# Routing in the attention loop: one TensorE product turns a row block back and gives its router logits, and VectorE adds the bias

## The reference

```
h = _layernorm(x) * (1 + cb) + sb
scores = softmax(h @ Wr + br)
_, top_idx = top_k(scores, 2)
weights = softmax(where(chosen, scores, -inf))
out = sum over the two experts of weights * (gelu(h @ W1 + b1) @ W2 + b2)
```

## Time and profile before

| | |
|---|---|
| median of three runs | 1105.14 us |
| span of the profiled execution | 1104.4 us |
| PE busy | 1019.0 us, 92% |
| DVE busy | 923.8 us, 84% |
| ACT busy | 969.8 us, 88% |
| POOL busy | 825.8 us, 75% |
| attention phase | about 30 to 815 us |
| granted PE clock from 60 to 800 us | 1.00 of full speed, 2.4 GHz |

### The profile page before, as it was taken

How to read it: one execution, slowest core, us unless ns; L and a number is a source line. 1 busy time by engine, 2 the same in 40 slices (tenths; PEclk the granted TensorE clock), 3 DMA queues, 4 the chain that set the end, 5 groups by cost and what they waited for, 6 DMA issues and landing times. The chain is left out here.

```text
span 1104.4 us, 27346 instructions
## 1 busy us (share of the span) xinstructions
PE 1019.0 (92%) x7434; PEld 791.3 (72%) x7434; DVE 923.8 (84%) x2706; ACT 969.8 (88%) x3517; POOL 825.8 (75%) x1197
## 2 busy tenths in 40 slices
PE   5899999999999999999999999999989999999800
PEld 3478888888888888888888888888865455579600
DVE  4888999989999999888888888888766997778837
ACT  6899999999999999999999999999769999999534
POOL 6665578888888888888878788888745687777744
PEclk9999999999999999999999999999999999999955
DMA  5320000001000000000000000000034233321158
GB/s 150 104 71 14 13 18 23 23 26 34 27 23 26 26 23 14 16 16 16 14 15 16 14 14 16 16 16 16 16 111 129 84 118 104 96 85 40 46 207 261
DMA packets 53704, 57.90 MB, mean 52 GB/s; under 512 B 7964, under 2 KB 42639, under 8 KB 53556
## 3 DMA queue, kind: packets, MB, share of 16 engines
q1 hardware_dynamic: 36468, 35.10, 10.9%
q0 software_dynamic: 8640, 16.87, 4.4%
q10 hardware_dynamic: 8448, 4.20, 1.3%
HBM read 33.08 MB, written 23.97 MB: 52 GB/s over the span
## 5 line engine op out<-in xcount | busy, mean ns | idle before, releaser
L751 ACT ACTIVATE squares<-unit 128x128 f32<-128x128 f32 x1024 | 273.0, 302 | 3.6 <-PE unit L1211 3.4
L563 POOL TENSOR_TENSOR roped<-roped,rope_b 128x512 f32<-128x512 f32 x132 | 174.9, 1326 | 93.8 <-DVE rope_b L1099 91.4
L751 ACT ACTIVATION_READ_ACCUMULATOR squares<-unit 128x1 f32 x1024 | 234.1, 235 | 0.0
L1080 DVE TENSOR_TENSOR roped<-unit,cos_sb 128x512 f32<-128x512 f32 x256 | 174.4, 681 | 31.7 <-ACT squares L751 30.9
L1563 POOL DMA_INDIRECT y_rows<-y_out,place_y x142 | 155.3, 1093 | 54.3 <-issue 40.5
L1099 DVE TENSOR_TENSOR rope_b<-unit,sin_sb 128x512 f32<-128x512 f32 x256 | 174.3, 681 | 0.0
L729 ACT ACTIVATE probs<-scores,rr 128x256 f32<-128x256 f32 x256 | 123.7, 483 | 51.6 <-issue 25.5
L1291 PEld LDWEIGHTS unit<-ident,roped 128*128 128x128 f32 x1024 | 117.9, 142 | 31.9 <-ACT k_t L768 13.1
L1049 DVE SCALAR_TENSOR_TENSOR acc<-pv,den,acc 128x128 f32<-128x128 f32 x448 | 139.0, 341 | 0.3
L1291 PE MATMUL unit<-ident,roped 128*128 128x128 f32 x1024 | 135.2, 275 | 1.7 <-POOL roped L563 1.6
L572 POOL TENSOR_TENSOR roped<-roped,rr 128x1024 f32<-128x1024 f32 x64 | 121.6, 1900 | 9.6 <-DVE roped L1108 8.8
(11 more groups left out here) (310 smaller groups left out, 2972.3 us busy)
## 6 DMA issues: line engine op xcount, KB each, us to landing
shared<-y_rows SPq DMA_DIRECT2D x16, 512.0 KB, 5.6
x_all<-in_L_attn_x SPq DMA_DIRECT2D x32, 128.0 KB, 2.1
h_late<-in_L_ffn_W SPq DMA_DIRECT2D x16, 256.0 KB, 3.5
out_x<-hidden ACTq DMA_DIRECT2D x16, 256.0 KB, 4.4
rope_b<-x_rows SPq DMA_DIRECT2D x13, 258.0 KB, 2.9
tile_x<-x_rows SPq DMA_DIRECT2D x12, 258.0 KB, 3.0
y_rows<-y_out,place_y POOLq DMA_INDIRECT x142, 2.3
ga_b<-mod_dram SPq DMA_DIRECT2D x32, 64.0 KB, 2.9
```

Source lines behind the costliest of these rows:

```text
L563: pool.tensor_tensor(out=roped[parity][:, u, heads], in0=roped[parity][:, u, heads], in1=rope_b[:, u % 2, heads], op=ALU.add)\
L751: nc.scalar.activation(squares[:, c * D:(c + 1) * D], UN[0][:, c * D:(c + 1) * D], ACT.Square, accum_out=ssq[parity][:, u * H + c:u * H + ...
L1080: nc.vector.tensor_tensor(out=roped[parity][:, u, heads].rearrange("p (g c) -> p g c", c=D // 2), in0=UN[0][:, heads].rearrange("p (g c) - ...
```

## The change

One product per 128-token block replaces three kinds of PE work. Its moving operand is a 128 x 136 tile, `ident_wr`, the identity with Wr beside it, so its output holds the turned block in columns 0 to 127 and the logits without bias in columns 128 to 135. Both products are issued right ahead of the values of heads 0 and 1, in slots 1 and 2, into columns 376 to 511 of banks pv0 and pv1. They stay there until `copy_rows` reads them, which remains in slots 4 and 5. DVE adds the bias with a new tile `br_all` (br on all partitions, one more DMA at the start) and writes the logits to a new SBUF tile `lg`; the steps behind read `lg`. In the code before they read PSUM. `ROUTE` moves several steps, ACT's exponential moves from slot 2 to slot 3, and POOL computes `h_lo` before `score`. Five small DVE instructions that split br at the start go.

```diff
+        lg = sb("lg", [P, TT, E])
...
-        BESIDE, TURN_AT = 2 * P + 8, 3 * P
+        BESIDE, TURN_AT = 2 * P + 8, 3 * P - E
...
+        ROUTED = {1: 0, 2: 1}
...
             ROUTE = {
-                (1, 0): (TOP_L0, TOP_L1), (1, 1): (LESS_TOP,), (3, 3): (E_SUM,), (3, 4): (E_REC,),
-                (5, 0): (TOP_S0, TOP_S1), (5, 1): (TOP_I0,), (5, 2): (TOP_I1,),
+                (1, 1): (BIASED0,), (2, 0): (BIASED1,), (2, 1): (TOP_L0, TOP_L1), (2, 3): (LESS_TOP,),
+                (4, 0): (E_SUM,), (4, 1): (E_REC,), (5, 1): (TOP_S0, TOP_S1), (5, 2): (TOP_I0,), (5, 3): (TOP_I1,),
                 (6, 1): (ONE_HOT,)}
...
-                    lg = OP[0][:, BESIDE:BESIDE + TT * E].rearrange("p (t e) -> p t e", t=TT)
...
+                    if step in (BIASED0, BIASED1):
+                        t = step - BIASED0
+                        wait(dve, "rt_done", TT * b + t + 1)
+                        ins = nc.vector.tensor_tensor(out=lg[:, t, :], in0=OP[t][:, TURN_AT + P:TURN_AT + P + E],
+                                                      in1=br_all[:, :], op=ALU.add)
...
                     elif step == LESS_TOP:
...
-                        ins = nc.vector.tensor_tensor(out=lg_m[:, :, :], in0=lg,
+                        ins = nc.vector.tensor_tensor(out=lg_m[:, :, :], in0=lg[:, :, :],
                                                       in1=top_l[:, :, 0:1].to_broadcast([P, TT, E]), op=ALU.subtract)
...
-                    if RT and h + 1 in BACK_AT:
-                        t = BACK_AT[h + 1]
+                    if RT and h + 1 in ROUTED:
+                        t = ROUTED[h + 1]
                         wait(pe, "h2t_copied", n - 4)
-                        nc.tensor.transpose(o[:, TURN_AT:TURN_AT + P], h2_t[:, t * P:(t + 1) * P], ident[:, :])\
-                            .then_inc(S["h2_back"], 1)
+                        wait(pe, "rows_copied", TT * (n - 5))
+                        wait(pe, "route_step", STEPS * (n - 6) + BIASED1)
+                        nc.tensor.matmul(o[:, TURN_AT:TURN_AT + P + E], h2_t[:, t * P:(t + 1) * P], ident_wr[:, :],
+                                         start=True, stop=True).then_inc(S["rt_done"], 1)
...
-                        for k in range(3):
-                            nc.tensor.matmul(dst, ones_bf[0:1, :], br_part[k][:, :], start=(k == 0), stop=False)
-                        for t in range(TT):
-                            ins = nc.tensor.matmul(dst[:, t * E:(t + 1) * E], h2_t[:, t * P:(t + 1) * P], wr_sb[:, :],
-                                                   start=False, stop=(t == TT - 1))
...
-                    if C and RT and h == 3:
-                        wait(pe, "route_step", STEPS * (n - 5) + LESS_TOP)
+                    if C and RT and h in (3, 4):
+                        wait(pe, "route_step", STEPS * (n - 5) + (BIASED0, BIASED1)[h - 3])
```

More of the change, by code:

```diff
@@ L98, in adaln_block @@
         mod_t = sb("mod_t", [P, 4, NB])
-        wr_sb = sb("wr_sb", [P, E])
         br_sb = sb("br_sb", [1, TT * E])
-        br_rest = [sb(f"br_rest{k}", [1, TT * E]) for k in range(2)]
-        br_part = [sb(f"br_part{k}", [1, TT * E], BF16) for k in range(3)]
+        br_all = sb("br_all", [P, E])
         ones_row = sb("ones_row", [1, P])
@@ L293, in iterations @@
                 body(n // 2, n % 2, live(n))
-        (TOP_L0, TOP_L1, LESS_TOP, E_SUM, E_REC, TOP_S0, TOP_S1, TOP_I0, TOP_I1, ONE_HOT) = range(1, 11)
+        (BIASED0, BIASED1, TOP_L0, TOP_L1, LESS_TOP, E_SUM, E_REC, TOP_S0, TOP_S1, TOP_I0, TOP_I1, ONE_HOT) = range(1, 13)
         STEPS = ONE_HOT
@@ L628, in body @@
                     scatter(n - 6, parity, 0, 0)
+                if X:
+                    b = n + 1
+                    wait(pool, "hhi_done", b + 1)
+                    wait(pool, "vw_done", TT * (b - 1))
+                    pool.tensor_tensor(out=h_lo[other][:, :], in0=h_t[:, :], in1=h_hi[other][:, :], op=ALU.subtract)\
+                        .then_inc(S["h_ready"], 1)
                 if RT:
@@ L634, in body @@
                                        op=ALU.mult).then_inc(S["scored"], 1)
[L635 to L640, removed]
                 if A:
@@ L777, in body @@
                             .then_inc(S["guess_done"], 1)
-                    if RT and h == 2:
+                    if RT and h == 3:
                         b = n - 5
@@ L819, in body @@
                         if not late:
-                            wait(act, "rt_done", b)
-                            wait(act, "h2_back", TT * b)
+                            wait(act, "rt_done", TT * b)
                         nc.scalar.activation(h2_late[:, b - LAST, :] if late else h2_t[:, :], UN[1][:, 0:T],
@@ L880, in biases @@
             def biases():
[L882 to L890, removed]
+                dve.wait_ge(S["router_in"], 16 * (TT + 2))
                 dve.wait_ge(S["b_turned"], 1)
@@ L956, in after @@
                         own(dve, "route_step", at + k)
-                    lg = OP[0][:, BESIDE:BESIDE + TT * E].rearrange("p (t e) -> p t e", t=TT)
-                    if step in (TOP_L0, TOP_L1):
+                    if step in (BIASED0, BIASED1):
[3 more added lines that the diff above has]
+                                                      in1=br_all[:, :], op=ALU.add)
+                    elif step in (TOP_L0, TOP_L1):
                         t = step - TOP_L0
-                        if t == 0:
-                            alone(dve, "rt_done", b + 1)
+                        after(BIASED0 + t)
                         ins = nc.vector.max(top_l[:, t, :], lg[:, t, :])
@@ L1022, in copy_rows @@
                     b, t = n - 5, BACK_AT[h]
-                    wait(dve, "h2_back", TT * b + h - H_AT + 1)
+                    wait(dve, "rt_done", TT * b + t + 1)
                     if (not isinstance(b, int) or b >= 2) and h == H_AT:
```

22 lines of the change are left out of this document (8 added, 14 removed).

## The result

The changed kernel is slower: 1118.09 us as the median of four runs (1117.49 to 1120.25), against 1105.7 us for the kernel before in the same comparison (1104.69 to 1106.32). The ratio is 1.0116, with an interval from 1.0104 to 1.0129. The forecast was 1099.6 us, faster, with a range of 1090 to 1117. The profiled span is 1116.5 us, 12.1 more than before.

A forecast was written before the change was run, and what follows sets the result against it. PE was taken to set the 24.56 us round, with a DVE and POOL ring equally long; -0.15 us in 25 rounds (-3.8) and -0.55 in three (-1.7) gave -5.5: 1098.9 in the profiled span, 1099.6 against the median, range 1090 to 1117.

The forecast's parts named there:

- PE's saving: PE, each routing round: -0.80 for small products, -0.22 for turns, +0.47 for new products; net -0.55 us (-0.58 to -0.42).
- rival (d): PE: small passes were nearly free, so the change saves no PE time; 1105 us, chance 0.04.
- The ring: DVE and POOL wait on each other in 24.56 us; PE's lead of 0.15 shrinks that to about 24.41.
- the slack of the earlier trace: Rounds from 19 on: DVE waits for ACT ahead of L1080 in slot 4, 0.36 us in round 25.
- The timing of the subtraction: DVE, slot 2: subtraction at 423.47, POOL's scaling L572 at 423.57 in round 17; late rounds counted on POOL being as late.
- DVE is first by 0.1 us, and the subtraction passes: Slot 2: the subtraction, with both inputs in SBUF, starts before POOL's L572 and is not held by the shared port.
- Rival (b): Slot 2: L572 holds the subtraction in all rounds from 7 on; +10 us, 1115, chance 0.22.
- the rounds that gain 0.55: Rounds 5, 6 and 32, without the scatter, gain PE's full 0.55 us each: -1.7 us in all.
- (a): PE stays the bound because the DVE and POOL waits fall elsewhere; 28 x -0.55 = -15.4 us, 1089, chance 0.15.
- (c): Slot 2: L572 holds the subtraction in the late rounds alone; +1 us, 1106, chance 0.17.
- Two other terms: Moved routing steps neither lengthen nor shorten DVE's dense stretch; PE's new waits name work DVE has already finished.

The follow-up runs named there:

- last experiment: Changed kernel with logits in PSUM, fourth scatter behind the first scaling and L620, first layer-norm statistics in slot 3 instead of 4: 1124.71 us, ratio 0.9878.
- first experiment: Changed kernel with the biased logits in spare columns of PSUM bank pv0 instead of the SBUF tile: 1130.65 us, ratio 0.993 against the kernel before.
- two more edits: On the changed kernel with logits in PSUM: fourth scatter moved behind the first scaling (ratio 0.9928), then also first statistics in slot 3 (0.9878).

## Why the prediction was wrong

- **PE's saving was right.** A pass of 136 columns takes 0.12 us (two passes, 0.24 from 422.45 to 422.69) against 0.117 forecast. Rounds 5 and 6, where nothing is held, are 0.40 us shorter in the changed kernel, not the 0.55 that I gave them, for some of PE's wait at heads 6 and 7 is there too; with the chain around it loosened the round is 0.52 to 0.56 us shorter (last experiment) against 0.55. That small float32 passes are not nearly free, the bet against rival (d), held.
- **The ring was right in kind.** I said that DVE and POOL would set the round and PE would wait for `acc` ahead of head 7. With the hold taken out (first experiment), the early round is 24.40 against 24.41 forecast, PE waits for `acc` ahead of head 7 (433.57), and POOL's L515 (L517 there) takes 0.55 us instead of 0.67. The late rounds were mis-sized: 24.19 instead of 24.41, so there the slack of the earlier trace rows let through 0.37 and not 0.15. With the hold in, PE waits first for L1096, in slots 4 and 5, a link that I hadn't named.
- **The timing of the subtraction was right in the early rounds.** I forecast a lead of 0.10 us over the scaling; it was 0.14 (428.82 against 428.96), and 0.13 in the first experiment, whose round has the forecast length. In rounds 19 to 30 the scaling came first, by 0.07 us. The forecast rested there on POOL being as late as in round 17, without a row for it.
- **The step that failed is "DVE is first by 0.1 us, and the subtraction passes".** I took the listed start of L572 as the moment at which it takes the lock. The instruction ahead of it is a scatter; with the scaling ready behind that, VectorE was refused 0.14 to 0.61 us before the scaling's listed start, the scatter then being 0.4 to 0.9 us under way. Two runs with 0.4 and 0.5 us of lead were held for the whole scaling; the run whose scaling was not yet free was not. No row of before showed this, since in none had a VectorE instruction with two SBUF inputs fallen into that gap. The nearest one misleads: the L1108 at 417.17 began 0.91 us into a scatter and 0.12 us ahead of the small L515, and passed in 0.69 us. I had not asked what POOL's instruction ahead of L572 was, and gave the forecast 0.42 on a margin of 0.1 us.
- **Rival (b) is what happened**, by its mechanism, with a chance of 0.22. It put the early round at 25.2, measured 25.13, and the late ones 0.25 to 0.4 over today, measured 0.35. Its sum of +10 came out as +12.1 in the span. The early rounds cost 6.8 us for 7.8, rounds 5 and 6 gave 0.8 for 1.1, and round 32, which I had put among the rounds that gain 0.55, lost 2.1: the subtraction stays held through both scalings there, 4.60 us. That this is the cause has no experiment of its own; where round 32 isn't held (the first experiment) it takes 20.04 us, against 20.00 before, so it had nothing to gain either.
- **Rivals (a) and (c).** (a), the ring giving way, didn't come by itself; it took two more edits. (c) called the late rounds held and the early ones free, but both were held. The late ones need no surprise: there the subtraction comes 0.07 us behind the scaling (1.87 us), while the early ones came ahead of it (2.09 us).
- Two other terms had no weight, as forecast: moving the steps with logits in PSUM gave a ratio of 0.9996, and PE has no wait for the new steps of the routing: its waits on DVE are 2.7 us in 14 pieces for `acc` and, at the weight loads, the 10.9 us for L1096.

Open: at which moment GpSimd begins to refuse. Arrivals 0.03 to 0.18 us into the scatter passed, those from 0.43 on were held where a scaling was ready behind it, and the runs don't say what happens inside GpSimd between. Nor is it shown why VectorE comes in between L575 and L623 in an ordinary round but not in round 32. There the second scaling follows L623 without a wait, where in an ordinary round it waits for L1105; this fits the other holds, but it is only argued.

## What to carry to other kernels

Moving a small operand from PSUM to SBUF can cost more than the PE time it saves: a VectorE instruction with two SBUF inputs may be held over several GpSimd instructions that are ready (4.60 us over three here), and all that stands behind it is held too. Before such a move, list what GpSimd runs at the instruction's new moment and what is queued behind that, and give the case no credit for a lead of tenths of a microsecond. Where the logits could stay, leaving one of the two inputs in PSUM cost nothing that the rounds show and was worth 0.73 us in each early round (25.13 to 24.40).

## What the runs showed of the hardware

- A large GpSimd instruction that is ready behind an indirect DMA holds VectorE while the DMA instruction is still listed as running: 2.48 us for 16 columns, begun 0.53 us ahead of the scaling. Without the ready instruction the same took 0.18 us. The Trainium skill ("SBUF — State Buffer", section "SBUF: two separate sides") says that whichever of the two starts first gets the pair for the whole instruction. The trace agrees on the lock and that it lasts to the end of the scaling (430.91 and 430.87), but not on who is first if listed starts are meant: the measurement decides, and a listed start behind an indirect DMA isn't when the lock is taken.
- A small GpSimd instruction behind a scatter did not hold VectorE 0.66 us into it (0.17 us), yet with a scaling behind the small one VectorE was held through both (2.52 us).
- Four passes of 128x8 in float32 and three products of one row cost 0.80 us of PE in a round, more than the 0.47 of two float32 products of 136 columns with all their passes. The four passes of 8 columns start 0.11 us apart, like those of 128, so their narrowness saved nothing. Each had its own load of 128x128 weights (four in 0.52 us), and the runs don't tell whether the pass or the load sets the 0.11 us.
